# Computing only the chosen token and expert pairs in four top-2 mixtures of a nine-block network

## The chip, the core and the metric

The program runs on one core of a Trainium2 chip. The metric is the time of one execution in microseconds (us), as the median of several runs. TensorE multiplies matrices, VectorE (DVE in the rows) and ScalarE (ACT) and GpSimd (POOL) work element by element, and SyncE (SP) issues all DMAs.

## The reference

A token grid of 16 x 16 with 192 channels (256 tokens) passes through four attention blocks and five mixtures of experts, in the order attention 0, mixture 0, attention 1, mixture 1, attention 2, attention 3, mixtures 2, 3 and 4. All is float32, and each block adds to the residual x after a layer norm. Every mixture has 8 routed experts of which each token takes the best 2. Mixture 0 reads (shortened):

```python
logits = x @ Wg; probs = softmax(logits)
top_vals, top_idx = top_k(probs, 2)
gates = (one_hot(top_idx, 8) * top_vals[..., None]).sum(-2)
h = relu(einsum('btc,ech->bteh', x, W1) + b1)      # C = 192, H = 768
y = einsum('bteh,ehc->btec', h, W2) + b2
out = einsum('bte,btec->btc', gates, y)
```

Mixture 1 is the same with a tanh GELU and gates normalised over the two. Mixture 2 gives every expert at most 64 tokens and drops the rest. Mixture 3 (GELU, biases) and mixture 4 (gated SiLU, hidden width 384, no biases) add a ninth, shared expert that every token takes. Only 512 of the 2048 token and expert pairs have a gate other than zero.

## The kernel before

One block follows another; within a block five instruction streams, one per engine, are written by hand and tied by semaphores. The loop over `BLOCKS` in each stream sets the order.

Mixtures 0, 1, 3 and 4 are dense: `expert(j, i)` runs every expert over all 256 tokens, two experts to a step of a hardware loop (`Fori`). For precision at one pass, each factor is split into a high and a low part of type float32r: ScalarE makes `w1_hi` (L613), VectorE `w1_lo` (L1363), GpSimd the two parts of half of w2 (L471, L473), VectorE those of the hidden layer (L1437, L1439). TensorE then does 30 matrix products of 256 columns per expert for the hidden layer (L1056), and the second layer in L1064, L1076 and L1078. VectorE adds the result times the gate to x (L1453, L1461). Two slots, `w1[0..1]` and `w2[0..1]`, hold the weights in turn, so an expert's weights stream in while the experts before are computed.

Mixture 2 (`places`) works on chosen pairs: VectorE turns the router's logits into the two picks (`sel`), TensorE counts how many earlier tokens picked each expert (L936 to L938), VectorE makes the 0/1 table `disp` of token against place (L1407), and a product with it gathers the tokens (L949) into `xdT`. Two experts of 64 places then share the 128 columns of the array (L964), the hidden layer is turned (L1005), goes through w2 (L1016), and a product with `combT`, the turned table of gates, puts it back to its tokens (L978). Its eight experts have eight slots of weights, six of them loaded during attention 2 and two during attention 3.

All DMAs go through one queue of SyncE, in the order of its stream. In attention 1 and 2 the queue carries `relall` to DRAM and back as `rel` (L370, L375), on which the queries wait.

Of the kernel before, what the change touches and what calls it, by code (L numbers as in the profile page):

```python
# [5 lines left out]
F32 = mybir.dt.float32  # L6
F32R = mybir.dt.float32r
U32 = mybir.dt.uint32
ALU = mybir.AluOpType
ACT = mybir.ActivationFunctionType  # L10
AX = mybir.AxisListType

# [20 lines left out]
SB = 2  # L33
SC = 2 * SB
CAP = 64
NEG = -3.0e38

# [3 lines left out]
for _name, _n in (("ident", P), ("earlier", P), ("ones", P), ("iota", E), ("onehot", TT * 2 * SIDE), ("rowhot", TT * SIDE), ("places", 64),  # L41
# [12 lines left out]
    dict(n=8, act="relu", split2=True, b=True, rbias=False, over_all=True, cap=False, eps=1e-5),  # L54
    dict(n=8, act="gelu_tanh", split2=True, b=True, rbias=True, over_all=False, cap=False, eps=1e-5),
    dict(n=8, act="gelu", split2=False, b=False, rbias=False, over_all=False, cap=True, eps=1e-5),
    dict(n=9, act="gelu", split2=True, b=True, rbias=False, over_all=False, cap=False, eps=1e-6),
    dict(n=9, act="glu", split2=False, b=False, rbias=True, over_all=False, cap=False, eps=1e-5),
)

BASE = [sum(m["n"] for m in MOE[:i] if not m["cap"]) for i in range(len(MOE) + 1)]
EP = E // 2


SHIFT = (0, 0, 0, 0, 1)
USED = ((0, 0), (4, 4), (8, 8), (9, 9), (14, 13))
# [7 lines left out]
def metaformer_kernel(nc, a, out):  # L74

    ctx = ExitStack()
    with ctx:
# [1564 lines left out]
```

## Time and profile before

| | |
|---|---|
| median of 3 runs | 462.65 us (462.55 to 463.0) |
| profiled execution: span | 461.0 us |
| TensorE, VectorE, ScalarE, GpSimd busy | 95%, 72%, 50%, 30% |
| TensorE's granted clock | full in all 40 slices |
| read from HBM, written | 59.82 MB, 2.10 MB |

The profiled execution's own time is its span, 461.0 us; the median of the runs is 1.65 us above it. The stages are told apart by the instructions that write x: mixture 0 runs from 41.7 to 109.3 us, mixture 1 from 146.6 to 214.2, mixture 2 from 287.2 to 327.1, mixture 3 to 401.5 and mixture 4 to the end. A busy share is how long at least one instruction of the engine was under way.

### The profile page before, as it was taken

The page shows a single profiled execution, that of the slowest core. Times are in us where ns is not written, and L with a number is a line of the kernel's source. Part 1 is how long each engine was busy: PE and PEld are TensorE (multiplying, and loading weights), DVE is VectorE, ACT ScalarE, POOL GpSimd, SP SyncE. Part 2 cuts the span into 40 slices and gives each one's busy share as a digit, 9 for nine tenths or more (in the row PEclk, how much of TensorE's full clock was granted, in tenths as well). Part 3 has the DMA queues.
Part 4 walks back from the last instruction along what each step waited for, and adds up shares of the span by engine and source line. Part 5 has one row for each costly group of instructions (what it writes and reads, how often), then busy time and mean ns, then how long its engine had stood idle before and what let it go on. Part 6 is the DMA issues. An engine that isn't in the chain of part 4 may idle for free.

```text
span 461.0 us, 9333 instructions
## 1 busy us (share of the span) xinstructions
PE 438.0 (95%) x3240; PEld 380.5 (83%) x3240; DVE 333.3 (72%) x756; ACT 232.7 (50%) x596; POOL 139.9 (30%) x178
## 2 busy tenths in 40 slices
PE   8999999999999999999999978899899999999997
PEld 7776999997676899998577756657699999879997
DVE  3775989995576989996475486511698999787774
ACT  1494455641295765642295275232284656365452
POOL 6012556561011465652001101200445665400000
PEclk9999999999999999999999999999999999999999
DMA  5560264710480155620389606005053756326650
GB/s 161 203 204 2 77 227 138 214 64 2 155 297 2 70 183 177 202 89 1 105 231 297 154 1 175 33 20 222 0 173 135 222 158 217 121 71 191 195 202 19
DMA packets 19365, 62.38 MB, mean 135 GB/s; under 512 B 4041, under 2 KB 6914, under 8 KB 19330
## 3 DMA queue, kind: packets, MB, share of 16 engines
q1 hardware_dynamic: 19330, 61.93, 42.5%
q8 instruction: 21, 0.34, 0.3%
q14 instruction: 14, 0.11, 0.1%
HBM read 59.82 MB, written 2.10 MB: 134 GB/s over the span
## 4 chain that ended last, share of the span: by engine, by line
PE 68%; issue 15%; ACT 6%; DVE 5%; POOL 3%; DMA 2%; POOLq 0%; SPq 0%; DVEq 0%
PE bank L1056 24%; PE bank L1064 10%; PE bank L1076 7%; ACT probs L574 5%; PE bank L724 4%; PE bank L1078 3%; PE bank L847 3%; PE bank L874 2%; PE bank L761 2%; DMA w<-in_M_w_dram 2%; PE bank L756 1%; PE bank L890 1%; POOL rstd L415 1%; PE bank L793 1%; PE bank L737 1%
## 5 line engine op out<-in xcount | busy, mean ns | idle before, releaser
L1056 PE MATMUL bank<-xT_hi,w_hi 128*128 128x256 f32 x408 | 109.2, 289 | 1.6 <-issue 1.6
L1363 DVE TENSOR_TENSOR w_lo<-w,w_hi 128x512 fp32r<-128x512 f32 x102 | 96.7, 987 | 2.3 <-ACT w_hi L613 0.4
L661 ACT ACTIVATE hid<-bank,b 128x256 f32<-128x256 f32 x150 | 62.7, 471 | 68.9 <-PE bank L1056 68.7
L1056 PE MATMUL bank<-xT_hi,w_lo 128*128 128x256 f32 x408 | 82.0, 282 | 0.0
L1056 PEld LDWEIGHTS bank<-xT_hi,w_hi 128*128 128x128 f32 x408 | 77.9, 191 | 3.9 <-issue 3.8
L471 POOL TENSOR_TENSOR w_hl<-w,consts 128x384 fp32r<-128x384 f32 x50 | 52.6, 1052 | 73.5 <-PE bank L1078 69.8
L1056 PEld LDWEIGHTS bank<-xT_hi,w_lo 128*128 128x128 f32 x408 | 63.4, 191 | 0.0
L473 POOL TENSOR_TENSOR w_hl<-w,w_hl 128x384 fp32r<-128x384 f32 x50 | 58.9, 1178 | 3.9
L1064 PE MATMUL bank<-w,hid 128*128 128x192 f32 x308 | 56.4, 327 | 2.3 <-issue 2.3
L613 ACT ACTIVATE w_hi<-w 128x512 fp32r<-128x512 f32 x102 | 58.3, 627 | 0.2 <-DMA w<-in_M_w_dram 0.2
L1056 PE MATMUL bank<-xT_lo,w_hi 128*128 128x256 f32 x204 | 57.7, 283 | 0.0
L1076 PE MATMUL bank<-w_hl,hid_hi 128*128 128x384 f32 x176 | 54.5, 375 | 0.0
L1064 PEld LDWEIGHTS bank<-w,hid 128*128 128x128 f32 x308 | 49.5, 190 | 3.5 <-issue 2.9
L1078 PE MATMUL bank<-w_hl,hid_lo 128*128 128x192 f32 x200 | 50.7, 254 | 0.0
L574 ACT ACTIVATE probs<-bank,nmax 128x256 f32<-128x256 f32 (+1 forms) x96 | 43.6, 493 | 11.0 <-DVE nmax L1308 6.7
L724 PE MATMUL bank<-warm 128*128 128x256 f32 x176 | 45.1, 398 | 1.2 <-DVE warm L1514 1.2
L452 POOL COPY rwide<-rinv 128x64 f32<-128x64 f32 x48 | 9.6, 237 | 102.9 <-DVE rinv L1321 99.7
L1056 PEld LDWEIGHTS bank<-xT_lo,w_hi 128*128 128x128 f32 x204 | 39.0, 191 | 0.0
L1078 PEld LDWEIGHTS bank<-w_hl,hid_lo 128*128 128x128 f32 x200 | 38.2, 191 | 0.0
L724 PEld LDWEIGHTS bank<-warm 128*128 128x128 f32 x176 | 33.3, 200 | 4.9 <-DVE warm L1514 1.2
L1439 DVE TENSOR_TENSOR hid_lo<-hid,hid_hi 128x512 fp32r<-128x512 f32 x50 | 34.6, 692 | 1.7
L1076 PEld LDWEIGHTS bank<-w_hl,hid_hi 128*128 128x128 f32 x176 | 33.0, 187 | 0.7
(178 smaller groups left out, 658.9 us busy)
## 6 DMA issues: line engine op xcount, KB each, us to landing
w<-in_M_w_dram SPq DMA_DIRECT2D x34, 768.0 KB, 5.5
w<-in_M_w_dram SPq DMA_DIRECT2D x33, 576.0 KB, 4.9
w<-in_M_w_dram SPq DMA_DIRECT2D x9, 288.0 KB, 2.8
wqkv<-in_A_wqkv_dram SPq DMA_DIRECT2D x4, 432.0 KB, 6.6
rel_scratch<-relall SPq DMA_DIRECT2D x4, 372.0 KB, 2.3
wproj<-in_A_wproj_dram SPq DMA_DIRECT2D x4, 288.0 KB, 7.4
wqkv<-in_M_w_dram SPq DMA_DIRECT2D x2, 576.0 KB, 21.1
rel<-rel_scratch SPq DMA_DIRECT2D x10, 96.0 KB
```

Of the source, the lines that this page charges most:

```text
L471: pool.tensor_tensor(parts[:, :, 0], w, one, ALU.mult).then_inc(w2_hi_ready, 1)
L473: pool.tensor_tensor(parts[:, :, 1], w, parts[:, :, 0].bitcast(F32), ALU.subtract).then_inc(w2_lo_ready, 1)
L574: act.activation(probs[:, p % 2, h, t, 0:keys_of(n, t)], scores_bank(p, h)[:, t, 0:keys_of(n, t)], ACT.Exp, bias=nmax[:, p % 2, h, t:t + 1 ...
L613: act.activation(w1_cols(w1_hi, b), w1_cols(w1[s], b), ACT.Copy).then_inc(w1_hi_ready, 1)
L661: ins = act.activation(hid[:, 2 * b + c, :], bank[B_H[b]][:, c * T:(c + 1) * T], FUNC[cfg["act"]], bias=b1[:, kb, bass.ds(at, 1)])
L724: pe.matmul(bank[b][:, 0:T], warm[:, 0:P], warm[:, :], start=True, stop=True)
L1056: ins = pe.matmul(bank[B_H[b]][:, c2 * T:(c2 + 1) * T], w, xs, start=(q == 0), stop=(q == 4))
L1064: ins = pe.matmul(bank[B_Y[t]][:, 0:C], hid[:, c, t * P:(t + 1) * P], w2[s][:, c * C:(c + 1) * C], start=(c == 0), stop=(c == nc2 - 1), sk ...
L1076: pe.matmul(out[:, 0:2 * C], hid_hi[:, c, tok], w2_hl[:, c].rearrange("p a n -> p (a n)"), start=False, stop=(c == SC - 1), skip_group_che ...
L1078: ins = pe.matmul(out[:, 0:C], hid_lo[:, c, tok], w2_hl[:, c, 0], start=False, stop=(c == SC - 1), skip_group_check=True)
L1363: dve.tensor_tensor(w1_cols(w1_lo, b), w1_cols(w1[s], b), w1_cols(w1_hi, b).bitcast(F32), ALU.subtract)\
L1439: dve.tensor_tensor(hid_lo[:, sb2:sb2 + 2, :], hid[:, 2 * b:2 * b + 2, :], hid_hi[:, sb2:sb2 + 2, :].bitcast(F32), ALU.subtract).then_inc( ...
```

## The change

In mixtures 0, 1, 3 and 4 only chosen pairs are computed, as in mixture 2, but without a limit per expert. There are 24 blocks of 32 tokens, in 6 units of 4 blocks; a unit fills the 128 columns of the array. Blocks 0 to 7 belong to experts 0 to 7 (units 0 and 1). The other 16 (units 2 to 5) are given at run time to the experts with more than 32 tokens: VectorE works out which expert owns each block and writes 16 offsets as integers (`w1_from`, `w2_from`); engines load them into registers. For each overflow unit the weights of its 4 blocks are copied within SBUF, from a register's address, into `stage1` (three blocks by VectorE, one by ScalarE) and `stage2` (all four by GpSimd, each block in two halves). All four overflow units are copied and computed whatever the routing. The high and low split is gone except for the gathering product; layers are plain float32. All eight experts' weights of a mixture are held at once in single buffers `w1` and `w2`: for mixtures 0, 1 and 2 three experts are loaded when the mixture before is done with them, the other five during attention; for mixture 3 during mixture 2; for mixture 4 when mixture 3 has made its last copy. The bias b1 becomes a 97th row of w1, turned on chip and sent through DRAM (`bias_rows`). The shared expert is computed densely in plain float32. Matrix products, copies and sums in the attention blocks are the same, with two slots for their weights in place of four.

```diff
@@ sizes
+BLK = 32
+PER = P // BLK
+STATIC = E * BLK
+OVER = 4 * P
+SLOTS = STATIC + OVER
+UNITS = SLOTS // P
+FIXED = STATIC // P
@@ SyncE
+            def weights_free(m):
+                last = staged(m, UNITS - 1, 1)
+                sp.wait_ge(st1_dve, last)
+                sp.wait_ge(st1_act, last)
+                sp.wait_ge(st2_pool, last)
...
+                if MOE[n]["b"]:
+                    bias_rows(n)
...
+                elif n < 4:
+                    weights_free(n)
+                    for e in range(E if n == 3 else early):
+                        load_expert(n + 1, e)
@@ GpSimd, in mixture(m)
+                for u in range(FIXED, UNITS):
+                    for half in range(2):
+                        if u > FIXED and half == 0:
+                            pool.wait_ge(yp_first, UB[m] + u)
+                        elif u > FIXED:
+                            pool.wait_ge(yp_psum, UB[m] + u)
+                        lo, hi = (0, cut) if half == 0 else (cut, cols)
+                        for k in range(PER):
+                            ins = pool.tensor_copy(stage2[:, k, lo:hi], flat[:, lo:][:, bass.ds(at[(u - FIXED) * PER + k], hi - lo)])
+                        ins.then_inc(st2_pool, 1)
@@ TensorE, in mixture(m, k)
+                def up(u):
+                    for c in range(KC):
...
+                            pe.wait_ge(st1_act, staged(m, u, c))
+                            pe.wait_ge(st1_dve, staged(m, u, c))
...
+                                ins = pe.matmul(bank[B_HP[u % 2][b]][q * BLK:(q + 1) * BLK, 0:HALF], xdT[0:kr, c, slot:slot + BLK], w,
+                                                start=(c == 0), stop=(c == KC - 1))
...
+                for u in range(UNITS):
+                    if u + 1 < UNITS:
+                        up(u + 1)
...
+                    turn_hidden(m, u)
+                    if u:
+                        add(u - 1)
...
+                    down(u)
@@ VectorE, in mixture(m)
+                for u in range(1, UNITS + 1):
+                    if glu and u < UNITS:
+                        hidden(u)
+                    ahead = u >= FIXED and u + 1 < UNITS
+                    if ahead:
+                        stage(u + 1, 0, 0, 1, 2)
+                        stage(u + 1, 1, 0)
+                    if not glu:
+                        hidden_turned(m, u - 1)
+                    if ahead:
+                        stage(u + 1, 1, 1, 2)
+                    out_placed(m, u - 1)
```

The rows that follow are instructions in each engine's own order. On GpSimd, mixture 0 before begins with the layer norm's power and the splits of w2 for two experts:

```order
L415 TENSOR_TENSOR rstd<-moments,minus_half 128x2
L471 TENSOR_TENSOR w_hl<-w_0,consts 128x2x192
L473 TENSOR_TENSOR w_hl<-w_0,w_hl 128x2x192
L471 TENSOR_TENSOR w_hl<-w_0,consts 128x2x192
L473 TENSOR_TENSOR w_hl<-w_0,w_hl 128x2x192
L471 TENSOR_TENSOR w_hl<-w_1,consts 128x2x192
L473 TENSOR_TENSOR w_hl<-w_1,w_hl 128x2x192
L471 TENSOR_TENSOR w_hl<-w_1,consts 128x2x192
L473 TENSOR_TENSOR w_hl<-w_1,w_hl 128x2x192
```

After, the same place ends the overflow part of the gate table, loads the offsets into registers, and copies w2 blocks (32 copies of 576 columns per mixture in all):

```order
L567 TENSOR_TENSOR comb<-comb,second_gate 128x512
L561 TENSOR_SCALAR comb<-iota_o,over_slot,pick_gate 128x512
L564 TENSOR_SCALAR second_gate<-iota_o,over_slot,pick_gate 128x512
L567 TENSOR_TENSOR comb<-comb,second_gate 128x512
L576 TENSOR_LOAD w_from
L576 ISA x32
L590 ISA
L590 COPY stage<-w 128x576
L590 ISA
L590 COPY stage<-w 128x576
L590 ISA
L590 COPY stage<-w 128x576
```

The splits, one set per expert, are gone, and copies that each have a register operation ahead stand in their place. On VectorE, mixture 0 before runs, for the second expert of its first pair and the next split:

```order
L1437 CAST hid_hi<-hid 128x512
L1439 TENSOR_TENSOR hid_lo<-hid,hid_hi 128x512
L1437 CAST hid_hi<-hid 128x512
L1439 TENSOR_TENSOR hid_lo<-hid,hid_hi 128x512
L1363 TENSOR_TENSOR w_lo<-w_0,w_hi 128x2x256 x3
L1453 SCALAR_TENSOR_TENSOR x<-bank,gates,x 128x192 x2
L1461 SCALAR_TENSOR_TENSOR x<-bank,gates,x 128x192 x2
```

After, this is one overflow unit but for the first of its six copies (`stage` is the staging tile; `hplaceT` is the turned hidden layer, `yplace` the unit's result):

```order
L1722 ISA
L1722 COPY stage<-w 96x768
L1722 ISA
L1722 COPY stage<-w 96x768
L1722 ISA
L1722 COPY stage<-w 97x768
L1596 COPY hplaceT<-bank 128x384
L1722 ISA
L1722 COPY stage<-w 97x768
L1722 ISA
L1722 COPY stage<-w 97x768
L1601 COPY yplace<-bank 128x192
```

Six copies of 768 columns now stand among the two instructions that TensorE waits for. On SyncE, before, the loop of mixture 0 ends with an expert's second matrix, and attention 1 sends and fetches the position terms and loads two experts behind them:

```order
L332 DMA w_1<-in_M_w_dram 128x1152
L399 REGISTER_ALU
L399 COMPARE_AND_BRANCH
L370 DMA rel_scratch<-relall 128x744 x2
L375 DMA rel<-rel_scratch 128x1x192 x4
L328 DMA w_0<-in_M_w_dram 128x1536
L332 DMA w_0<-in_M_w_dram 128x1152
L328 DMA w_1<-in_M_w_dram 128x1536
```

After, at the same place, the weights of three experts of mixture 1 stand ahead of the position terms; these are the last of them:

```order
L358 DMA w<-in_M_w_dram 64x768
L368 DMA w<-in_M_w_dram 128x1152
L356 DMA w<-in_M_w_dram 96x768
L357 DMA w<-in_M_w_dram 32x768
L358 DMA w<-in_M_w_dram 64x768
L368 DMA w<-in_M_w_dram 128x1152
L432 DMA rel_scratch<-relall 128x744 x2
L437 DMA rel<-rel_scratch 128x1x192 x4
```

The four rows ahead of `rel_scratch` repeat for each of those three experts.

## Rows read from the trace of the kernel before

**Rows 1.** The page: busy share, granted clock, chain by line

```profile
PE 438.0 (95%) x3240; PEld 380.5 (83%) x3240; DVE 333.3 (72%) x756; ACT 232.7 (50%) x596; POOL 139.9 (30%) x178
...
PEclk9999999999999999999999999999999999999999
...
PE bank L1056 24%; PE bank L1064 10%; PE bank L1076 7%; ACT probs L574 5%; PE bank L724 4%; PE bank L1078 3%; PE bank L847 3%; PE bank L874 2%; PE bank L761 2%; DMA w<-in_M_w_dram 2%; PE bank L756 1%; PE bank L890 1%; POOL rstd L415 1%; PE bank L793 1%; PE bank L737 1%
```

**Rows 2.** Busy time by stage: mixtures 0, 1, 3 and 4

```profile
41.70:109.30 67.60, 65.48 (x477) 63.30 (x476) 60.44 (x121) 32.93 (x75) 36.38 (x33) 1.00 0.39 123
...
146.60:214.20 67.60, 65.49 (x477) 63.30 (x476) 60.44 (x121) 36.80 (x78) 36.34 (x33) 1.00 0.38 123
...
327.10:401.50 74.40, 71.97 (x527) 69.75 (x526) 66.81 (x131) 41.14 (x89) 40.95 (x37) 1.00 0.48 155
401.50:461.00 59.50, 55.54 (x402) 53.26 (x400) 41.56 (x103) 28.41 (x59) 1.04 (x1) 1.00 0.42 136
```

**Rows 3.** Timeline from 285 us (start, length, engine): mixture 2's routing, first products

```profile
285.04 0.86 PE L890 MATMUL bank<-pT,v_st 128*32 128x256 f32 x16
...
292.47 0.17 DVE L1377 COPY logits<-bank 128x16 f32<-128x16 f32 x1 [1.21 <-PE bank L1033]
...
295.64 1.29 DVE L1407 TENSOR_TENSOR w_hi<-consts,place 128x512 fp32r<-128x512 f32 x2
...
296.48 2.06 PE L949 MATMUL bank<-w_hi,w_lo 128*96 128x512 f32 x8 [0.23 <-DVE w_hi L1407]
...
299.53 2.80 PE L964 MATMUL bank<-w,pT 96*64 96x384 f32 x16 [0.99 <-ACT pT L618]
...
302.26 1.09 PE L992 MATMUL bank<-consts,probs 128*128 128x128 f32 x8
```

**Rows 4.** Groups by line and form (count, busy us, mean ns)

```profile
L613 ACT ACTIVATE w_hi<-w 128x512 fp32r<-128x512 f32 x102 | 58.3, 627 | 0.2 <-DMA w<-in_M_w_dram 0.2
...
L1437 DVE CAST hid_hi<-hid 128x512 fp32r<-128x512 f32 x50 | 21.9, 437 | 11.0 <-ACT hid L661 10.5
...
L625 ACT ACTIVATE hplace<-bank 128x384 f32<-128x384 f32 x8 | 3.6, 492 | 1.3 <-PE bank L964 1.3
...
L1486 DVE COPY q_st<-bank 128x384 f32<-128x384 f32 x4 | 2.2, 558 | 9.3 <-PE bank L1005 9.3
...
L504 POOL TENSOR_TENSOR probs<-w_hi,gates 128x512 f32<-128x512 f32 x2 | 2.0, 1042 | 5.4 <-DVE gates L1420 5.4
...
L431 POOL COPY k_st<-consts 128x384 f32<-128x384 f32 x2 | 1.0, 504 | 0.3 <-DMA consts<-in_consts_dram 0.3
```

**Rows 5.** L1363 (minimum/median/maximum ns), and two rows of the timeline

```profile
L1363 DVE TENSOR_TENSOR w_lo<-w,w_hi x102: 646/693/1506, 43.1 to 451.8; 128x512 fp32r<-128x512 f32 x102
...
69.92 3.34 DVE L1363 TENSOR_TENSOR w_lo<-w,w_hi 128x512 fp32r<-128x512 f32 x3
...
71.37 1.34 POOL L473 TENSOR_TENSOR w_hl<-w,w_hl 128x384 fp32r<-128x384 f32 x1
```

**Rows 6.** A register operation on GpSimd's queue (minimum/median/maximum ns)

```profile
L472 POOLq FUSED_REGOPS  x18: 37/37/43, 62.9 to 384.1; - x18
```

**Rows 7.** DMA in two stretches of attention 2, and one issue's landing

```profile
236.00:240.00 4.00, 3.66 (x30) 2.72 (x28) 3.21 (x7) 4.00 (x16) 0.41 (x2) 1.00 1.01 324
...
224.00:228.00 4.00, 3.46 (x23) 2.63 (x21) 2.50 (x8) 1.20 (x2) 0.00 (x0) 1.00 0.47 144
...
bqkv<-in_M_w_dram SPq DMA_DIRECT2D x1, 576.0 KB, 23.7
```

**Rows 8.** SyncE's issues (attention 0, 1, mixture 2), the chain in attention 2

```profile
17.13 0.33 SPq L328 DMA_DIRECT2D w<-in_M_w_dram  x1
...
116.63 1.57 SPq L370 DMA_DIRECT2D rel_scratch<-relall  x2
...
309.35 0.35 SPq L328 DMA_DIRECT2D w<-in_M_w_dram  x1
...
228.07 0.85 PE bank L817 x6
```

More of the change, by code:

```diff
@@ L161, in metaformer_kernel @@
         gates = sb("gates", [P, TT, E + 1])
[L162 to L171 removed]
+        longer = sb("longer", [P, E, E - 1])
@@ new lines, in dispatch @@
+            def dispatch(m, t, banks, cols, done):
+                for c in range(KC):
+                    for q, part in enumerate((xn_hi, xn_lo)):
+                        if q == 1:
+                            pe.wait_ge(xn_lo_ready, m + 1)
+                        ins = pe.matmul(banks[c], part[:, t, c * CH:(c + 1) * CH], disp[:, t, cols],
+                                        start=(t == 0 and q == 0), stop=(t == TT - 1 and q == 1), skip_group_check=True)
+                if t == TT - 1:
+                    ins.then_inc(done, 1)
@@ new lines, in turn_hidden, with capacity @@
+            def turn_hidden(m, u):
+                n = chunks(m) // HB
+                for b in range(n):
+                    pe.wait_ge(hp_ready, 2 * (UB[m] + u) + (b + 1 if n == 2 else 2))
+                    for c in range(HB):
+                        ins = pe.transpose(bank[B_HT[b]][:, c * P:(c + 1) * P], hplace[:, (b * HB + c) * P:(b * HB + c + 1) * P], ident)
+                    ins.then_inc(hpT_psum, 3 - n)
+            def capacity(m, k):
+                router(m, k)
+                stay_warm(5)
+                positions(m)
@@ L1509, in moe, with capacity @@
[L1509 to L1512 removed]
+                    at.append(own[0])
+                return at
+            def capacity(m):
+                selection(m)
+                places(m, CAP)
+                gate_sums(m)
+                gate(m)
+                dve.wait_ge(xd_psum, m + 1)
+                dve.tensor_scalar(xdT[0:CH, 1, 0:E * CAP], bank[B_XD[1]][0:CH, :], lnw[:, 1, 1:2], None, ALU.mult).then_inc(xd_dve, 1)
+                dve.wait_ge(pcT_psum, 1)
+                dve.tensor_copy(combT[:, 0:2, :].rearrange("p a t -> p (a t)"), bank[B_HT[0]][:, :]).then_inc(pcT_dve, 1)
+                then(dve.tensor_tensor(x[:, :, :], x[:, :, :], tln[:, :, :], ALU.add))
+                for ep in range(EP):
+                    hidden_turned(m, ep)
+                    out_placed(m, ep)
+                settle()
+                return summed(m)
```

1217 lines of the change are left out of this document (662 added, 555 removed).

## The prediction

> **What bounds the kernel now.** I read the page first: TensorE is busy 95% of the span, its clock is full in every slice, and the chain that ends last is a third on L1056 and L1064, the dense layers [rows 1]. Then the busy time by stage: in mixtures 0, 1 and 3 TensorE is busy in all but 2 us or so, VectorE is close behind with the splits, GpSimd at half [rows 2]. These stages and mixture 4 take 67.6 + 67.6 + 74.4 + 59.5 = 269.1 of 461.0 us. Less TensorE work shortens them as far as nothing else is put in its place, so I price the new form from mixture 2, which already works on chosen pairs [rows 3], and ask which engine ends last.
>
> **TensorE's new work per unit.** In L964 two experts share the array: 16 products of 384 columns take 2.80 us, 0.35 per pair. With 32-column tiles L890 does 16 products of 256 columns in 0.86 us, 0.22 per round of four [rows 3]. So up(u), 4 rounds of 384 columns, costs 1.4 us; down(u), 6 rounds of 192 at half that, 1.05; six turns at 0.136 (8 in 1.09) 0.8; add(u) 0.35. Sum 3.6 us a unit, 22 for six: one dense expert costs about twice a unit, since eight fill 67.6 us.
>
> **The staging per overflow unit.** GpSimd makes 8 copies of 576 columns. Its copy of 384 takes 504 ns [rows 4]; 576 take between that and 756, and since a small copy has a fixed part (0.17 us even for 16 columns on VectorE [rows 3]), I take 0.66 and 0.61 from start to start: 4.9 us. VectorE makes 6 copies of 768; its cast of 512 from SBUF to SBUF takes 437 ns against 693 for two inputs [rows 4, 5], so a one-input copy runs at about double the rate per column, and 768 cost 0.5 us from start to start: 3.0 us, plus the turned half (0.56) and the result (0.36) and small waits: 4.2. ScalarE: two hidden halves and a turned half at 0.49 and two copies of 768 at 0.8 (512 take 627): 3.1 us [rows 4]. A register operation takes 37 ns on GpSimd's queue [rows 6] and lies beside the copies. What a register as address adds to a copy has no row: below nothing, above what (E) below works with; I take 0.
>
> **Do the copies add up?** Where VectorE and GpSimd both work from SBUF, they hold each other up: three w_lo take 3.34 us beside GpSimd's splits, against 0.65 each alone, and GpSimd's own instruction beside them takes 1.34 [rows 5]. These have two inputs; for one-input copies at double rate the trace has no overlap. Bounds: no hold-up, a unit takes 4.9 (GpSimd alone); full, 4.9 + 6 x 0.42 = 7.4. I take full hold-up, by the nearest row. The Trainium skill, SBUF — State Buffer, "Who interferes with whom", says that a VectorE instruction in a two-port mode and a GpSimd one exclude each other for their whole length, copies included; no run here shows it yet.
>
> The orders confirm that they overlap: GpSimd's next block halves wait only for down of the unit before, VectorE's stage for the same up, and hidden_turned stands behind four of the six copies, so down's second half waits for VectorE too. Stepping through four units from X, when GpSimd may start: T2 = X+7.4; down(2) waits for up(3) and its turn and starts at X+9; then GpSimd ends at X+17, X+23 and X+28 (no VectorE staging beside the last), and 2 us of down, result, add and sum follow: **X+30**. Without hold-up the same steps give X+23.6.
>
> **X, mixture 1.** In mixture 2, x is complete at 287.8 (its window's start and 0.6), disp starts at 295.6 and the first up at 299.5 [rows 3]. Here disp has 256 columns (2 x 0.42), the gathering product 1.0, xdT 0.8, up(0) 1.4: 12.1. VectorE meanwhile runs some 20 small routing instructions at 0.2 (0.17 each for the smallest [rows 3]) and 4 of 512 columns (0.45 and 0.69): overflow disp is ready at 14.0, its product (2.06 for eight [rows 3]) ends at 15.0. Then comb turned 1.1, biases 0.4, up(1) 1.4, turn and copy 1.3, down(0) 1.1, overflow comb turned 1.1: 21.5. GpSimd's table (two of 512 at 0.62 and a two-input at 1.04 [rows 4], twice) ends at 19.6, beside that. Loading 16 offsets on VectorE and GpSimd and four on ScalarE has no row: at least the 32 register operations at 0.04, 1.3 us, mostly hidden; at most 5, if each of ScalarE's four loads took what VectorE's place table does (1.29 [rows 3]). I take 2, nearer to the register row: X = 23.5, the mixture 53.5 after x, 54.1 in its window. The Trainium skill, Runtime: NRT & Kernel Launch, gives about 200 ns per register loaded from HBM; by that 16 would take 3.2 us, an estimate, and the sum would be 1 us a mixture longer.
>
> **The other mixtures: DMA.** The one queue moves 324 GB/s when full, and 144 at 0.47 of full, about 300 either way; it is first in, first out, a 576 KB load behind eleven others landing after 23.7 us [rows 7]. Mixture 0: eight experts (9.4 MB) and attention 1's weights (1.2 MB) are issued from 17 us on [rows 8] and end at 53; the bias, turned after the router at 47, goes behind them and back in by 56.5, 3 us after up(0) wants it: 2 us on X, window 56.1. Mixture 3: its loads go behind mixture 2's downs from 309.4 on, as two of them do now [rows 8], and 9.4 MB end at 342; the bias rows wait behind them and are back at 345, 5 to 6 us after up(0) wants them: X = 28.8, 58.8 us. Mixture 4: 7.1 MB start 2 us before mixture 3 ends and take 23.6 us; up(1) waits until 22, X = 26; with three chunks GpSimd copies 3.0 us a unit, with hold-up 5.5: X+22 = 48, and 2.2 to the end as now: 50.2.
>
> Attention 1 and 2: three experts (3.5 MB, 11.8 us) are ahead of the position terms. These are issued at 116.6, 7.3 us after x [rows 8]; after, they move at 10. The queries start right behind the values product, without a wait [rows 8], so there is little cover: +2.5 us each (bounds 0 and 4), 5 in all.
>
> **Sum.** 461.0 - (67.6 - 56.1) - (67.6 - 54.1) - (74.4 - 58.8) - (59.5 - 50.2) + 5 = 461.0 - 49.9 + 5 = 416.1, against the profiled execution; the median of the runs lay 1.65 us above it: **418 us**.
>
> **Rivals.** (A) The forecast, staging with hold-up, 405 to 430: 0.45. (B) No hold-up between one-input copies: four chains 6.4 shorter, 392 (385 to 405). For: no row shows it for copies. Against: rows 5. 0.15. (C) TensorE's clock falls. It is at 2.4 GHz in all slices while busy 95% [rows 1]; in the staging stretches it would work 3.6 us in 7.4, idle up to 3 us at a time. At 1.2 GHz its part doubles: up, turn, half a down and their copies lie between GpSimd's halves, +1.5 us a unit, 16 units, 24 us: 442 (430 to 448). The Trainium skill, TensorE: Matmul & The Clock Gate, Part 1, calls the low clock the default that activity lifts; that speaks for (C). 0.20. (D) DMA at 3 KB rows is slower, say 200 GB/s: mixture 4 waits 12 us longer, 3 and 0 about 6 each: 442. Against: the position terms' short rows move at the same full rate [rows 7]. 0.08. (E) Slower than before: GpSimd's register-addressed copies. The gain of 45 us over 16 units is 2.8 us a unit, 0.35 a copy; if each needs 1.1 us from start to start in place of 0.61 (its two-input instruction of 384 took up to 1.34 [rows 5]) and holds VectorE as long, a unit takes over 11 us and the time is 470 or more. It decides from 0.35 us a copy on. 0.07, and 0.04 for 442 to 461 by a milder form. That the pairs are not fewer is excluded: the order lists the products.
>
> **Range and chances.** The range goes from 393 to 444: it leaves out the low part of (B), half of the tail of (C) and all of (E), about 2 in 10. A measurement tells 0.2% of the time, 0.9 us, from no change. Faster: A, B, C, D and most of the milder tail, 0.92; same 0.01; slower 0.07.
>
> **What would show it.** GpSimd's COPY of stage at about 0.66 us alone and more beside VectorE's; VectorE's 96x768 copies at 0.56 alone; mixtures of 54 to 59 us between writes of x; products waiting for GpSimd's stage in units 3 to 5; the clock below full in mixtures for (C); w DMAs landing later than 24 us into mixture 4 for (D). I am wrong if the chain in the overflow units runs through another engine, or the lead-in is longer than 24 us in mixture 1.

## The result

The changed kernel takes 489.35 us (median of 4 runs, 487.6 to 497.14), the kernel before 462.8 beside it: a ratio of 1.0568 (95% interval 1.0547 to 1.059). It is slower; the prediction said 418 us. Ratios leave out runs in a slower state, which medians keep: 497.14 here, two of four of b_noregs and one of four each of c_half, d_onepick and e_nostage, whose medians without them are 489.25, 476.67, 477.84, 489.71 and 465.39. The profiled execution has a span of 487.4 us, 26.4 above the 461.0 of before.

The page after the change: busy times, the granted clock in 40 slices and the chain by line, to be read beside [rows 1].

```profile
PE 412.6 (85%) x3753; PEld 284.3 (58%) x3753; DVE 239.7 (49%) x639; ACT 165.6 (34%) x432; POOL 173.9 (36%) x254
...
PEclk9999768998999998999999999999998899887899
...
PE bank L1213 9%; POOL stage L590 6%; PE bank L1235 6%; DMA bias_scratch<-b1T 5%; DVE stage L1722 3%; DMA w<-in_M_w_dram 3%; DVEq L1706 2%; PE bank L840 2%; SPq L357 2%; SPq L358 2%; PE bank L1076 2%; SPq L356 2%; SPq L368 2%; PE bank L1111 2%; DMA rel_scratch<-relall 2%
```

TensorE's busy time fell by only 25 us, its idle time rose by 52, and the clock is no longer full. The chain, a third of which was two matrix lines, is now spread over copies, DMAs and register instructions.

Busy time by stage after the change (window, length, then TensorE, its weight loads, VectorE, ScalarE, GpSimd, the granted clock, DMA share, GB/s): mixture 0, attention 1, mixture 1, attentions 2 and 3, mixtures 2, 3 and 4. The rows of before are [rows 2].

```profile
41.90:119.50 77.60, 57.87 (x626) 37.64 (x625) 33.40 (x88) 17.44 (x35) 38.47 (x43) 0.88 0.25 63
119.50:159.70 40.20, 36.57 (x250) 26.71 (x249) 22.52 (x57) 19.12 (x65) 3.13 (x13) 0.98 0.89 256
159.70:224.20 64.50, 54.73 (x628) 36.57 (x627) 33.68 (x89) 18.60 (x36) 40.19 (x43) 0.97 0.11 28
224.20:263.80 39.60, 35.96 (x248) 25.77 (x248) 22.56 (x57) 20.40 (x66) 3.12 (x13) 1.00 0.90 259
263.80:301.20 37.40, 31.19 (x236) 23.68 (x235) 23.18 (x76) 17.64 (x64) 4.46 (x15) 1.00 0.08 16
301.20:340.50 39.30, 37.13 (x265) 25.43 (x264) 11.73 (x41) 9.32 (x20) 3.73 (x4) 1.00 0.60 175
340.50:419.50 79.00, 64.28 (x659) 43.52 (x658) 33.50 (x89) 22.41 (x43) 38.44 (x43) 0.92 0.27 67
419.50:487.40 67.90, 55.55 (x477) 34.41 (x475) 33.67 (x90) 18.40 (x32) 28.36 (x42) 0.88 0.38 101
```

| us | before | forecast | after |
|---|---|---|---|
| mixture 0 | 67.6 | 56.1 | 77.6 |
| mixture 1 | 67.6 | 54.1 | 64.5 |
| mixture 3 | 74.4 | 58.8 | 79.0 |
| mixture 4 | 59.5 | 50.2 | 67.9 |
| attentions 1, 2, 3 | 110.3 | 115.3 | 117.2 |

Of the four mixtures only mixture 1 gained. The four mixtures lie 69.8 us above the forecast, of 71.3 in all.

Mixture 1, timeline of the lead-in (x is complete at 159.7): start, length, engine.

```profile
173.90 2.09 POOL L561 TENSOR_SCALAR comb<-iota_o,over_slot,pick_gate 128x512 f32<-128x512 f32 x1 [4.07 <-DVE pick_gate L1679]
...
176.32 2.79 PE L1213 MATMUL bank<-w,xdT 96*32 96x384 f32 x32
...
181.57 3.88 POOL L564 TENSOR_SCALAR second_gate<-iota_o,over_slot,pick_gate 128x512 f32<-128x512 f32 x1
181.66 3.32 DVE L1722 COPY stage<-w 96x768 f32 x6 [5.23 <-issue]
184.91 0.54 DVE L1596 COPY hplaceT<-bank 128x384 f32<-128x384 f32 x1
185.51 1.97 PE L1235 MATMUL bank<-w,hplaceT 128*32 128x192 f32 x24 [3.22 <-DVE hplaceT L1596]
185.53 1.27 POOL L567 TENSOR_TENSOR comb<-comb,second_gate 128x512 f32<-128x512 f32 x1
187.41 1.93 PE L1325 MATMUL bank<-consts,comb 128*128 128x128 f32 x8
...
189.26 2.79 PE L1213 MATMUL bank<-stage,xdT 96*32 96x384 f32 x32
...
191.02 2.40 POOL L590 COPY stage<-w 128x576 f32 x2 [4.22 <-issue]
```

Four things stand here (a record is one matrix instruction in the trace, a product one in the program). An up is 32 records, not 16, and takes 2.79 us. GpSimd's two-operation instruction of the gate table takes 2.1 us, and 3.9 beside VectorE's copies. VectorE idles 5.23 us with no releaser ("issue"), then makes its six copies, and only then copies the turned half on which the second half of down(0) has waited 3.22 us. And both paths, GpSimd's table and down(0), end together: 186.8 and 187.4. The first overflow up starts 29.6 us after x, GpSimd's first copy 31.3 us after it: behind the table it loads 16 registers of its own, 4.2 us. That end was hidden, since down of that unit, at 200.75, waited only for ScalarE.

What VectorE does in those 5 us (minimum/median/maximum ns) stands on its queue: one load of 16 offsets, 1.10 us, then 16 register operations of 0.18 and 16 bounds tests of 0.02, with gaps 4.4 us; the load began beside the copy before, so VectorE's idle time is 5.2 and not 5.5.

```profile
L1706 DVEq FUSED_REGOPS  x64: 183/183/206, 72.1 to 446.7; - x64
L1706 DVEq SEQ_ASSERT  x64: 23/23/41, 72.4 to 446.9; - x64
L1706 DVEq TENSOR_LOAD <-w_from x4: 1096/1102/1349, 70.8 to 441.4; - x4
```

The overflow units of mixture 1, timeline: from 195.98 to 202.69 and 209.87 one unit takes 6.7 and 7.2 us.

```profile
195.98 2.79 PE L1213 MATMUL bank<-stage,xdT 96*32 96x384 f32 x32
...
198.70 0.88 PE L1087 MATMUL bank<-consts,hplace 128*128 128x128 f32 x6
...
199.41 0.82 PE L1250 MATMUL bank<-yplace,combT 128*128 128x192 f32 x4
...
200.75 2.16 PE L1235 MATMUL bank<-stage,hplaceT 128*32 128x192 f32 x48 [0.52 <-ACT hplaceT L727]
202.11 11.91 POOL L590 COPY stage<-w 128x576 f32 x16 [3.97 <-PE bank L1235]
...
215.99 4.93 POOL L590 COPY stage<-w 128x576 f32 x8 [1.96 <-PE bank L1235]
```

TensorE works through a unit with one gap of 0.52 us, for ScalarE. GpSimd's eight copies take 4.93 us alone, 0.61 each, and 11.91 for sixteen beside VectorE's, 6.0 a unit.

Mixtures 0, 3 and 4 add waits for DMAs. Their first products after the wait, in the timeline:

```profile
63.93 2.79 PE L1213 MATMUL bank<-w,xdT 97*32 97x384 f32 x16 [10.07 <-DMA w<-bias_scratch]
...
363.35 2.79 PE L1213 MATMUL bank<-w,xdT 97*32 97x384 f32 x16 [5.07 <-DMA w<-bias_scratch]
...
445.18 5.35 PE L1213 MATMUL bank<-w,xdT 96*32 96x384 f32 x32 [3.83 <-DMA w<-in_M_w_dram]
```

The chain that ended last has the biases' way out and back in mixture 0, and in attention 3 the layer norm's weights (start, length):

```profile
52.51 8.51 DMA bias_scratch<-b1T
61.03 2.66 DMA w<-bias_scratch
...
261.24 10.23 DMA lnw<-in_lnw_dram
```

And three stretches, with the columns of the stages: mixture 0 at the end of the wait and behind it, and mixture 3's weights arriving (full clock is 1.00, 2.4 GHz; 0.50 is 1.2 GHz):

```profile
60.00:64.00 4.00, 0.07 (x4) 0.10 (x8) 0.00 (x0) 0.00 (x0) 3.81 (x4) 0.50 0.03 6
67.00:71.00 4.00, 4.00 (x16) 2.78 (x15) 0.69 (x2) 1.24 (x3) 0.21 (x1) 0.66 0.03 6
...
340.00:345.00 5.00, 4.36 (x27) 3.41 (x25) 2.42 (x9) 0.81 (x2) 2.40 (x3) 1.00 1.04 258
```

The clock is at half in the wait, and the 16 records of the second half of up(0) then take 2.79 us, as long as 32 at full clock. The DMA engines move 258 GB/s at a full share here.

### The profile page after: what moved, and what is told of

Same layout as the page of the kernel before. It is cut to its first block, busy times and chain, and to the rows that moved or that the text cites. A ratio compares the mean times of both kernels' runs of the same rounds, so it can differ in the third digit from the quotient of the medians.

```text
span 487.4 us, 10115 instructions
## 1 busy us (share of the span) xinstructions
PE 412.6 (85%) x3753; PEld 284.3 (58%) x3753; DVE 239.7 (49%) x639; ACT 165.6 (34%) x432; POOL 173.9 (36%) x254
## 4 chain that ended last, share of the span: by engine, by line
PE 39%; DMA 15%; SPq 15%; DVE 8%; issue 7%; POOL 7%; ACT 5%; DVEq 3%; POOLq 0%; ACTq 0%
PE bank L1213 9%; POOL stage L590 6%; PE bank L1235 6%; DMA bias_scratch<-b1T 5%; DVE stage L1722 3%; DMA w<-in_M_w_dram 3%; DVEq L1706 2%; PE bank L840 2%; SPq L357 2%; SPq L358 2%; PE bank L1076 2%; SPq L356 2%; SPq L368 2%; PE bank L1111 2%; DMA rel_scratch<-relall 2%
## 5 line engine op out<-in xcount | busy, mean ns | idle before, releaser
L590 POOL COPY stage<-w 128x576 f32 (+2 forms) x128 | 86.5, 724 | 74.6 <-PE bank L1325 37.9
L1722 DVE COPY stage<-w 96x768 f32 (+1 forms) x96 | 60.9, 693 | 30.4 <-issue 21.6
L1213 PE MATMUL bank<-stage,xdT 96*32 96x384 f32 (+1 forms) x512 | 45.1, 487 | 2.8 <-DVE stage L1722 2.8
L1213 PE MATMUL bank<-w,xdT 96*32 96x384 f32 (+1 forms) x256 | 27.9, 578 | 20.4 <-DMA w<-bias_scratch 15.1
L1235 PE MATMUL bank<-stage,hplaceT 128*32 128x192 f32 x672 | 32.1, 329 | 10.7 <-POOL stage L590 6.0
L722 ACT ACTIVATE hplace<-bank 128x384 f32<-128x384 f32 x44 | 19.6, 489 | 62.6 <-PE bank L1087 35.3
L791 ACT ACTIVATE stage<-w 96x768 f32 (+1 forms) x32 | 26.7, 846 | 29.8 <-PE bank L1213 29.8
L1235 PEld LDWEIGHTS bank<-stage,hplaceT 128*32 128x32 f32 x672 | 22.1, 109 | 19.4 <-POOL stage L590 12.2
L1235 PE MATMUL bank<-w,hplaceT 128*32 128x192 f32 x336 | 19.6, 382 | 15.2 <-DVE hplaceT L1596 9.4
L963 PE MATMUL bank<-kT,qT 64*128 64x256 f32 (+1 forms) x192 | 24.9, 384 | 3.7 <-ACT probs L669 2.4
L990 PE MATMUL bank<-consts,probs 128*128 128x128 f32 x180 | 25.5, 279 | 2.4 <-issue 1.1
L990 PEld LDWEIGHTS bank<-consts,probs 128*128 128x128 f32 x180 | 19.5, 141 | 10.1 <-ACT pT L682 5.8
L1485 DVE TENSOR_REDUCE nmax<-bank 128x2 f32<-128x512 f32 x36 | 22.5, 682 | 4.0 <-PE bank L963 3.9
```

Source lines behind the costliest of these rows:

```text
L590: ins = pool.tensor_copy(stage2[:, k, lo:hi], flat[:, lo:][:, bass.ds(at[(u - FIXED) * PER + k], hi - lo)])
L722: act.activation(hplace[:, half * HALF:(half + 1) * HALF], hp, FUNC[MOE[m]["act"]]).then_inc(hp_ready, 1)
L791: act.activation(stage1[0:rows, PER - 1, lo:lo + HID], flat[0:rows, lo:][:, bass.ds(regs[u - FIXED], HID)], ACT.Copy)\
L963: ins = pe.matmul(scores_bank(p, h)[:, t, 0:keys_of(n, t)], qT[head_rows(h), p, t * P:(t + 1) * P], kT[head_rows(h), p, 0:keys_of(n, t)], ...
L990: ins = pe.transpose(bank[B_PT[kt]][:, h * T + t * P:h * T + (t + 1) * P], probs[:, p % 2, h, t, kt * P:(kt + 1) * P], ident)
L1213: ins = pe.matmul(bank[B_HP[u % 2][b]][q * BLK:(q + 1) * BLK, 0:HALF], xdT[0:kr, c, slot:slot + BLK], w, start=(c == 0), stop=(c == KC - 1))
```

## The experiments

Each experiment up to h_v1 is measured against the median of 489.35 or the one named. Wherever a kernel uses other experts' weights or leaves out columns, its expectation says so.

**a_bias: biases loaded as rows**

```diff
-                sp.wait_ge(b1_turned, k + 1)
-                sp.dma_start(bias_scratch[k], b1T[:, :]).then_inc(b1_out, 16)
-                sp.wait_ge(b1_out, 16 * (k + 1))
-                sp.dma_start(w1[CH:CH + 1, :, HID:2 * HID], bias_scratch[k]...)
+                sp.dma_start(w1[CH:CH + 1, :, HID:2 * HID], a[f"M{m}_b1rows"]...)
```

> The rows of b1 come from the host in the layout of the weights and are loaded beside them, so that nothing is turned and nothing goes through DRAM; the output is the same. Theory 1 (the biases' round trip behind the weight loads is on the path): up(0) waited 10.1 us in mixture 0 (idle before L1213 at 63.93) and in mixture 3 the path lay on the trip from 345.4 to 363.4, of which 351 on is wait, 12 us; each wait also sends TensorE's clock to half for some 10 us, 2 to 3 us more each. Together 24 to 28 us: 460 to 464. Theory 2 (the wait only covers what the register loads and the gate table would cost anyway): the same shortening of the wait, but the mixtures gain 5 us or less each: 477 to 487.

474.6 us (ratio to before 1.0215 to 1.0313): 15 us, between the two. Mixture 0 went from 77.6 to 67.2 and mixture 3 from 79.0 to 71.6. Both gained more than theory 2 allows, and together 17.8 and not theory 1's 24 to 28: the round trip is on the path, but smaller than I had it. In mixture 3 I had counted as wait the shared expert's work, which TensorE does meanwhile.

**b_noregs: fixed addresses in place of register loads**

```diff
-                _, regs = nc.values_load_multi_w_load_instructions(w1_from[0:1, :], ...)
+                regs = [i % E * KC * HID for i in range(BLOCKS_OVER)]
```

> No offset is loaded into a register, and every staging copy reads from a fixed address; the overflow blocks so use the weights of experts in a fixed order, not of their owners. Theory 1 (register loads lie beside GpSimd's gate table, which ends at the same time): 1 to 2 us a mixture, 479 to 483, and a GpSimd copy of 576 stays at 0.61 us alone. Theory 2 (the register loads on VectorE, 5.2 us a mixture, are what holds the first down): 4 to 5 us a mixture, 467 to 471. Theory 3 (a register as address slows each copy): the medians of the copies fall by 0.1 us or more and the time goes below 465.

480.55 us, but its four runs go from 473.91 to 484.99, too far apart to tell theory 1 from something between the two. GpSimd's and VectorE's groups of copies (count, busy us, mean ns), fixed addresses first, then the changed kernel's:

```profile
L589 POOL COPY stage<-w 128x576 f32<-128x576 f32 x96 | 72.0, 800 | 45.6 <-PE bank L1233 23.1 <-PE bank L1323 22.6
L1719 DVE COPY stage<-w 96x768 f32<-96x768 f32 x60 | 39.6, 718 | 14.8 <-PE bank L1211 9.0 <-DMA w<-in_M_w_dram 5.7
```

```profile
L590 POOL COPY stage<-w 128x576 f32 x96 | 72.0, 798 | 55.9 <-PE bank L1325 31.2 <-PE bank L1235 20.5 <-issue 4.2
L1722 DVE COPY stage<-w 96x768 f32 x60 | 37.9, 688 | 30.4 <-issue 21.6 <-PE bank L1213 8.8
```

800 against 798 ns and 718 against 688: a register as address costs a copy nothing. Theory 3 falls, and with it rival (E). Mixture 1 gained 0.4 us, as theory 1 has it; mixtures 0 and 3, where the register loads come behind the bias wait and GpSimd's table is long done, gained 5.3 and 6.2, theory 2's size.

**c_half: half of TensorE's columns**

```diff
-  ... bank[B_HP[u % 2][b]][q * BLK:(q + 1) * BLK, 0:HALF], xdT[...], w[..., b * HALF:(b + 1) * HALF]
+  ... bank[B_HP[u % 2][b]][q * BLK:(q + 1) * BLK, 0:HALF // 2], xdT[...], w[..., b * HALF:b * HALF + HALF // 2]
```

> TensorE computes only half of the columns of each product of up and down in the four routed mixtures (the other half of the hidden layer and of the result is left as it was in the banks); all copies stay. Theory 1 (TensorE's 6.7 us a unit sets the pace of the overflow units): a unit goes to 5 to 6 us, where GpSimd's copies then hold it, and two ups and a down in the lead-in give 3.5 us: 7 us or more a mixture, 455 to 460. Theory 2 (staging sets the pace as forecast, 7 us a unit whatever TensorE does): only the lead-in gains, 3 to 4 us a mixture, 471 to 476.

478.64 us. GpSimd in mixture 1, timeline:

```profile
186.81 20.73 POOL L590 COPY stage<-w 128x576 f32 x24 [4.23 <-issue]
```

24 copies without a pause take 20.73 us, 6.9 a unit: staging with hold-up, which the prediction put at 7.4, now sets the pace, as theory 2 has it. It is only just behind TensorE's 6.7. Mixture 1 gained 2.2 us, less than theory 2's 3 to 4, and the whole lies above theory 2's 471 to 476, with runs from 472.49 to 485.09. The clock fell too: 0.87 against 0.97 in mixture 1, 0.83 against 0.88 in mixture 0.

**d_onepick and f_both: the gate table alone, and with the register loads**

```diff
-                    then(pool.tensor_scalar(second_gate[:, :], iota_o[:, :], over_slot[:, t, 1:2], pick_gate[:, t, 1:2], ...))
-                    settle()
-                    ins = pool.tensor_tensor(part, part, second_gate[:, :], ALU.add)
```

> GpSimd makes the overflow part of the gate table from the first pick alone (one instruction of 512 columns for each half of the tokens in place of three); the second pick's gates are left out of the overflow blocks. It is then done 9 us earlier. Theory 1 (down(0) behind VectorE's register loads ends at the same time as the table): little, 1 to 2 us a mixture and only by less contention, 479 to 484. Theory 2 (GpSimd's table sets the start of the overflow units): 5 to 6 us a mixture, 464 to 468.

> Both at once: no offset is loaded into a register (fixed addresses, so other experts' weights in the overflow blocks), and GpSimd makes the gate table from the first pick alone. Alone the one gave 10 us, none of it in mixture 1, and the other nothing. Theory 1 (in the lead-in two paths of equal length run side by side, VectorE's register loads ahead of the first turned hidden layer and GpSimd's table): mixture 1 now goes from 64.5 to 58 to 60 us, and the whole to 460 to 468. Theory 2 (something else holds the first overflow unit, the cuts are hidden anyway): mixture 1 stays above 63, the whole at 476 to 482.

d_onepick took 489.93 us, no gain, and f_both 474.88 (473.53 to 476.35), which the scattered runs of b_noregs don't set apart from it. The stages do. In mixture 1 the first gave 0.5 us, b_noregs 0.4, and both together 4.8 (59.7 us). Theory 1 holds for the place: two paths of equal length, of which either alone hides the other. The whole missed its range of 460 to 468: mixtures 0, 3 and 4, which wait for DMAs besides, were only 0.2 to 0.9 us shorter than in b_noregs, and attention 1 took 43.4 us in place of 40.2.

**e_nostage: no staging copies**

```diff
-  w = (w1[0:kr, u * PER + q] if u < FIXED else stage1[0:kr, q])[:, c * HID:(c + 1) * HID]
+  w = w1[0:kr, (u * PER + q) % E][:, c * HID:(c + 1) * HID]
...
-  w = w2[:, u * PER + q] if u < FIXED else stage2[:, q]
+  w = w2[:, (u * PER + q) % E]
```

> No staging copy is made; the overflow units read the weights of experts in a fixed order straight from where the DMAs put them, so the overflow part of the output is that of other experts. The register loads and all else stay. Theory 1 (once under way, TensorE's own chain of 6.7 us a unit is as long as the staging; only the last units and the first down wait for copies): 5 to 7 us a mixture, 460 to 467. Theory 2 (the working of the prediction: staging holds each unit at 7.4 us and TensorE needs 3.6): some 15 us a mixture, below 435. In a unit the chain then shows up, turn, add and down of 2.8, 0.9, 0.8 and 2.2 us without a gap over 0.5 us for theory 1.

466.24 us: theory 1. The prediction's own working, theory 2, is refuted by 30 us: with no copy left, mixture 1 still takes 58.8. All copies together cost 23 us here.

**g_split: w1 loads start before the last w2 copies**

```diff
-                    weights_free(n)
-                    for e in range(E if n == 3 else early):
-                        load_expert(n + 1, e)
+                    for which in ("w1", "w2"):
+                        weights_free(n, which)
+                        for e in range(E if n == 3 else early):
+                            load_expert(n + 1, e, (which,))
```

> The biases come with the weights as in a_bias, and SyncE issues the next mixture's w1 as soon as the last copies out of w1 are made, its w2 after GpSimd's last copies; the output is the same. Against a_bias (474.6): theory 1 (mixture 4 waits for its weights, 7.1 MB at 265 GB/s from the end of mixture 3's last copy): the w1 DMAs start some 7 us earlier, mixture 4 goes from 69.4 to 62 to 65 us, attentions 1 and 2 gain 1 us each: 466 to 469. Theory 2 (mixture 4's start is held by routing and tables, not by the weights): 473 to 476.

462.78 us (0.9988 to 1.004, no different from before), 12 under a_bias and better than either theory. Mixture 4 went from 69.4 to 65.3, at the edge of theory 1, and attentions 1 and 2 from 41.5 and 41.0 to 38.4 each, more than its 1 us.

**l_warm: products in the bias waits** of the changed kernel

```diff
+                            if u == 0 and c and m in (0, 3):
+                                stay_warm({0: 20, 3: 10}[m], 3)
```

> The kernel after the change, with the same output, and 20 products of 256 columns on constants between the two halves of up(0) in mixture 0 (9.3 us, where TensorE waits 10.1 us for the bias rows) and 10 in mixture 3 (4.6 us in a wait of 5.1). Theory 1 (a wait lowers the granted clock, which then costs its own time): the second half of up(0) takes 1.5 us in place of 2.79, the overflow dispatch 2.0 in place of 3.0, together 2 to 3 us in mixture 0 and in mixture 3: 482 to 485. Theory 2 (the slower clock is hidden behind VectorE's and GpSimd's tables and register loads, which do not run on it): less than 1 us each, 487 to 490.

484.34 us. Mixture 0, timeline:

```profile
62.87 1.50 PE L1215 MATMUL bank<-w,xdT 97*32 97x384 f32 x16
```

1.50 us in place of 2.79; mixture 0 went from 77.6 to 73.4, mixture 3 from 79.0 to 76.6. Theory 1: a wait costs its length and then the clock behind it.

**h_v1: a shorter lead-in**

```diff
+  act.activation(comb[:, t, STATIC:SLOTS], disp[:, t, STATIC:SLOTS].bitcast(F32), ACT.Copy, scale=pick_gate[:, t, 1:2])
+  act.activation(first_over[:, t, :], first_over[:, t, :], ACT.Copy, scale=more_gate[:, t:t + 1])
+  pool.tensor_tensor(part, part, first_over[:, t, :], ALU.add)
...
+                load_regs(FIXED)
                 stage(FIXED, 0, 0, 1, 2)
-                stage(FIXED, 1, 0, 1, 2)
...
                     hidden_turned(m, u - 1)
+                    if not glu and u == 1:
+                        stage(FIXED, 1, 0, 1, 2)
```

> The output is the same. Biases and early w1 loads as in g_split; the layer norm's weights for attention 3 are loaded an attention earlier; ScalarE makes the two products of the overflow gate table (table times gate) and GpSimd only adds them; VectorE loads three registers a unit, without a bounds test, and copies the first turned hidden layer after three of its first six copies. Theory 1 (the time went into the lead-in of each mixture): the first overflow up comes at 24 to 26 us after x in place of 29.6, each mixture is 4 to 6 us shorter than in g_split: 443 to 452, under the kernel before. Theory 2 (staging takes it back: the same copies start earlier and end as late, or a slower clock takes the rest): 458 to 468.

`load_regs` loads three registers, for one unit; the `tensor_tensor` is all that GpSimd keeps of the table.

**440.22 us, a ratio of 0.952 (0.9504 to 0.9535)**: theory 1, a little better than its 443 to 452, and faster than the kernel before. Its stages, mixtures 0, 1, 3 and 4:

```profile
41.90:101.40 59.50, 52.91 (x627) 35.85 (x626) 35.60 (x90) 19.50 (x38) 30.50 (x39) 1.00 0.42 113
139.60:199.00 59.40, 52.84 (x627) 35.77 (x626) 35.39 (x89) 20.90 (x39) 30.46 (x39) 1.00 0.23 60
311.80:376.40 64.60, 58.44 (x659) 41.15 (x658) 35.54 (x90) 24.70 (x46) 30.71 (x39) 1.00 0.51 127
376.40:438.60 62.20, 52.87 (x476) 32.79 (x474) 34.38 (x92) 20.75 (x36) 20.27 (x38) 0.92 0.23 67
```

And its lead-in in mixture 1, timeline:

```profile
157.08 3.50 DVE L1724 COPY stage<-w 96x768 f32 x3 [0.82 <-issue]
...
164.05 2.79 PE L1209 MATMUL bank<-stage,xdT 96*32 96x384 f32 x32
```

VectorE idles 0.82 us for registers in place of 5.23, the first overflow up starts 24.4 us after x in place of 29.6, and the clock is full. The edits came together: against g_split they give 22.6 us, and what each gives was not measured.

**i_tail, j_order, k_all: the last unit's copies shared, ScalarE's order, both**

```diff
-                        for k in range(PER):
+                        for k in range(PER if u < UNITS - 1 else PER - 2):
...
+                    hidden_turned(m, u - 1)
                     for half in range(1 if glu else 2):
                         hidden(m, u, half)
-                    hidden_turned(m, u - 1)
...
+                    act.activation(stage2[:, PER - 1, lo:hi], flat2[:, lo:][:, bass.ds(reg2, hi - lo)], ACT.Copy).then_inc(st2_act, 1)
...
+                        dve.tensor_copy(stage2[:, PER - 2, 0:cut2], flat2[:, bass.ds(reg2, cut2)]).then_inc(st2_dve, 1)
```

> As h_v1, and of the last unit's w2 blocks GpSimd copies two, VectorE one and ScalarE one; the output is the same. Theory 1 (after the last up only GpSimd's two halves of 2.45 us are left, and TensorE waits for them): each half takes 1.25 us, the idle before the last downs (0.3 and 1.25 us in mixture 1) goes, 1.5 to 2.5 us a mixture but for mixture 4, where the copies are smaller: 432 to 436. Theory 2 (the three engines' copies from one memory hold each other up and end as late as one engine's): 438 to 442.

> As h_v1, but ScalarE copies the turned hidden layer of a unit before it makes the hidden layer of the next; the output is the same. Theory 1 (TensorE's own chain bounds the overflow units: it waits 0.52 us before each down for that copy, which stands behind 0.87 us of hidden layer): 0.5 us a unit, 24 units, 428 to 432. Theory 2 (staging holds the units at 6.9 us whatever TensorE does): the wait moves to GpSimd's stage, and at most 2 to 4 us in all are gained, 436 to 439.

> Both edits, of i_tail and j_order, on h_v1; the output is the same. If each works by itself the gains add: 424 to 430. If GpSimd's copies bound the units once TensorE waits less, the two together give what the tail gives and little more: 432 to 436.

(The second piece is j_order's, the others are i_tail's.) 436.02, 439.41 and 436.28 us. Mixture 1 took 57.5, 57.2 and 55.3 us against 59.4: each edit gives 2 us there and they add, as theory 1 of each has it. In the whole only i_tail comes to its theory 1, at the edge; j_order (428 to 432 wanted) and k_all (424 to 430) miss theirs and end at or just above the ranges for little gain (436 to 439, 432 to 436), though mixture 1 speaks for theory 1. Mixture 4 in k_all, and in i_tail:

```profile
364.90:436.20 71.30, 57.33 (x475) 34.50 (x474) 35.96 (x93) 21.22 (x38) 20.29 (x34) 0.85 0.25 68
```

```profile
371.00:431.90 60.90, 48.25 (x476) 30.10 (x474) 36.21 (x94) 21.43 (x38) 20.19 (x34) 1.00 0.28 78
```

10.4 us more at a clock of 0.85. These two executions are the slowest of k_all and the fastest of i_tail, while the medians lie 0.3 us apart; but j_order's mixture 4, at 67.8 us and 0.90, and h_v1's, at 62.2 and 0.92, point the same way. The four runs of k_all go the same way, from 433.84 us at a mean clock of 0.986 to 438.01 at 0.976.

**o_all_warm: products in mixture 4's waits**

```diff
+                    if glu and 1 < u < UNITS - 1:
+                        stay_warm(2, 6)
```

> k_all with the same output and two products on constants in mixture 4 behind the positions and ahead of each up of units 3 to 5, where TensorE waits for VectorE's copies. In k_all mixtures 0, 1 and 3 kept the gains of both edits (59.5, 59.4 and 64.6 us in h_v1, 55.6, 55.3 and 60.8 in k_all), and mixture 4 took 71.3 us at a granted clock of 0.85 against 60.9 at 1.00 in i_tail. Theory 1 (short waits in mixture 4 let the clock fall, and products in them keep it up): mixture 4 at 59 to 61 us and the whole at 424 to 428. Theory 2 (the clock of mixture 4 falls whatever TensorE does in its waits): 432 to 438.

433.01 us, **0.9359 of before (0.9346 to 0.9372), the fastest version with the right output**. Two stretches of mixture 4 (length, TensorE, clock, DMA share, GB/s):

```profile
390.00:400.00 10.00, 8.32 (x94) 1.00 0.00 0
400.00:410.00 10.00, 8.12 (x77) 0.85 0.01 2
```

The whole lies in the range of theory 2. Mixture 4 took 67.4 us at 0.92, not 59 to 61; its clock was full to 400 us and 0.78 to 0.85 after it, at the same busy share. The products gained 3.3 us, and what lowers the clock in the late units stays open.

**m_v1half and n_v1nostage: h_v1 with half the columns, and without copies** (the edits of c_half and e_nostage)

> h_v1 with only half of the columns of each product of up and down in the routed mixtures computed (the rest of the hidden layer and of the result is left as it was), all copies kept: TensorE's work per unit is then about what the prediction took. Theory 1 (the prediction's count of TensorE's work was half of the true one, and this is what is left between 440 and its 418): the lead-in and the last unit gain 1.4 + 1.4 + 1.0 us and 1 us, 5 us a mixture, and the units stay at GpSimd's 6.9 us: 418 to 424. Theory 2 (with less to do TensorE's clock falls to half in the waits and gives the gain back): 430 to 442, the granted clock under 0.9 in the mixtures.

> h_v1 without any staging copy; overflow units use the weights of experts in a fixed order where they lie. Theory 1 (in mixtures 0, 1 and 3 TensorE's chain of 6.7 us a unit is the bound, staging costs the tail only): mixture 1 goes from 59.4 to 55.5 to 57, mixture 4, whose TensorE waits for VectorE's copies, from 62.2 to 53 to 56: 418 to 426. Theory 2 (staging holds every unit): mixture 1 under 52, the whole under 408.

422.6 and 423.74 us. GpSimd in mixture 1 of m_v1half, timeline, and the stages of mixture 1 and 4 of n_v1nostage:

```profile
157.90 7.35 POOL L586 COPY stage<-w 128x576 f32 x8 [3.39 <-PE bank L1318]
167.66 11.98 POOL L586 COPY stage<-w 128x576 f32 x16 [2.40 <-PE bank L1231]
```

```profile
137.40:194.30 56.90, 52.41 (x627) 35.09 (x626) 18.67 (x66) 14.61 (x31) 6.13 (x7) 1.00 0.23 59
...
369.30:421.70 52.40, 46.76 (x475) 30.00 (x473) 19.42 (x67) 14.82 (x28) 5.40 (x6) 1.00 0.36 100
```

With TensorE at the prediction's own size the kernel takes 422.6, theory 1: the 17.6 us between it and h_v1 are the price of that count. The clock fell to 0.85 to 0.94 in the four mixtures, the mechanism of theory 2, but took only part back. n_v1nostage is theory 1 as well: all staging is worth 16.5 us, 2.5 of them in mixture 1 and 9.8 in mixture 4 (52.4 us in place of 62.2), where the clock is full again and not 0.92.

## Why the prediction was wrong

- **"16 products ... 0.22 per round of four [rows 3]. So up(u), 4 rounds of 384 columns, costs 1.4 us"** failed. The rows' x16 count records, and a float32 product leaves two ([rows 3]: L964 has 8 products and 16 records); a turn leaves one, so that the turns, forecast at 0.8 and measured at 0.88, were right. (Of L890's 16 records 8 have 128 columns, so that row was no round price either.) I took a time per record and multiplied by products. An up is 32 records, 8 rounds of 0.35 us, 2.79; a down 2.16 in place of 1.05; an add 0.82 in place of 0.35; a unit 6.7 in place of 3.6. It was worth some 10.7 us in the changed kernel (c_half) and 17.6 once the waits were gone (m_v1half); more is hidden, since staging holds a unit at 6.9 anyway.
- **"GpSimd's table (two of 512 at 0.62 and a two-input at 1.04 [rows 4], twice) ends at 19.6"** failed: 0.62 was priced from a plain copy, and an instruction with two per-token operands takes 2.07 alone (3.88 beside VectorE's copies). The table ended 27 us after x. "I take 2" for the register loads failed beside it: 5.2 us on VectorE, 0.27 per register and 1.1 for the load, just over the upper bound of 5 that I had named, and not hidden, since the turned half stood behind it. Shortening either alone gave nothing in mixture 1, both 5 us (f_both, h_v1). X was 31.3, the table's 27.1 and 4.2 for GpSimd's own register loads, not 23.5. The Trainium skill, Runtime: NRT & Kernel Launch, "Instruction fetch mechanics", gives about 200 ns per register for a TENSOR_LOAD from HBM; here the offsets lie in SBUF, 16 of them load in 1.10 us, 0.07 each, and most of the time is the 0.27 per register of operation, test and gaps behind it.
- **"Behind them and back in by 56.5, 3 us after up(0) wants it"** was mis-sized: TensorE waited 10.1 us in mixture 0. The round trip through DRAM took 8.5 us out, behind weights that arrived at some 260 GB/s and not 300, and 2.7 back. With the slower clock behind the waits the round trips of all mixtures cost 15 us (a_bias).
- **"Up(1) waits until 22"** in mixture 4: 25.7 us after x, for the same rate. Starting w1 early gave 12 us in all, 4.1 of them in mixture 4.
- **Attention +5** was right in size: +2.9 and +1.9. Attention 3 took 2.1 more, which I had not looked for: its layer norm weights, issued at 261.24, landed at 271.5.
- **Hold-up** was right in kind and a little large: 7.4 a unit forecast, 6.9 in c_half, 7.35 for the first and 6.0 for each of the next two in m_v1half; 0.61 us a copy alone was exact, and the copy's register address adds nothing. By the Trainium skill, SBUF — State Buffer, "Who interferes with whom", a VectorE copy in a two-port mode and a GpSimd one exclude each other. The traces agree in direction: in c_half the 18 copies of VectorE beside them made GpSimd's three units 20.73 us in place of 3 x 4.93, 0.33 us for each. But staging didn't set the pace of the units, as TensorE's own 6.7 us a unit was as long.
- **The rivals.** (C) was the nearest in kind, not in place: in the changed kernel the clock fell in and behind the waits for DMAs and tables (l_warm: 5 us). Where TensorE had only the forecast's work, it fell more: to 0.87 in mixture 1 of c_half, to 0.91 to 0.94 in mixtures 0, 1 and 3 of m_v1half, and there in (C)'s own place: 0.66 from 175 to 180 us, behind 2.86 us of waiting for GpSimd's copies. (B) falls by the hold-up. (D) came in part: 258 to 265 GB/s at a full share, not 200. (E) gave the right side by luck, for a wrong reason.

Taken out one after the other, the bias round trip (14.8 us), the late w1 (11.8), the edits of h_v1 (22.6) and the miscount (17.6) bring the time from 489.35 to 422.6, 5 us from the forecast. In another order each would have another price, as f_both shows.

The staged sum had nearly each number from a row, but all these misses point one way: a unit of count, a cheap row for an unseen instruction, the lower end for an unseen load, a transfer rate from another mix of transfers.

## What to carry to other kernels

Before a time per record is multiplied, count the records of one known instruction in the trace against the program's listing: here float32 products left two, turns one. When work moves into fewer products, add up what now runs ahead of the first one, path by path; two hidden paths of equal length look free one at a time and must be shortened together. Weights copied on chip from a register's address cost no more than from a fixed one; register loads in a lead-in were cheap once VectorE loaded only three at a time, just ahead of use (0.82 us of idle time in place of 5.23 in h_v1).

## What was not expected of the hardware

- An instruction of GpSimd with two per-token scalars on 128x512 takes 2.07 us, a scaled copy of the same size on ScalarE, which does only the multiplication, 0.71 (h_v1).
- A register loaded on VectorE took 0.27 us (0.18 the operation, 0.02 the test) and one load of 16 offsets 1.10; on GpSimd 0.15 for the operation.
- A wait of 10 us left TensorE at half clock at its end, and at a mean of 0.66 from 67 to 71 us though busy throughout; twenty products in the wait kept it full (l_warm, 54 to 71 us).
- With nothing else changed but half of TensorE's columns, the granted clock of mixture 1 went from 1.00 to 0.93 (h_v1, m_v1half).
